# The last tile's chain in two column halves on VectorE, and the unpacking of a 4-bit matrix in another place

## What is computed

```python
c = attention(x, Wq, Wk, Wv, Wo, ...)              # 8 x 128 x 512
s = silu(c @ w_gate.T)                             # 1376 columns
s[the 688 columns of each row with the smallest |s|] = 0
x = x + (s * (c @ w_up.T)) @ w_down.T              # "x1" below
y = x @ weight[adapter_id].T                       # adapter, one of 16 matrices per batch
x = x + y @ W.T + b                                # W, b unpacked: (packed >> 4 & 15, packed & 15) - 8, times a scale
```

## Time and profile before

| | us |
|---|---|
| median of 3 runs (range) | 1464.77 (1464.52 to 1466.59) |
| the profiled execution | 1462.63 |
| its span, first to last instruction | 1460.8 |
| TensorE busy | 1405.2 (96%) |
| VectorE busy | 1184.6 (81%) |
| ScalarE busy | 873.3 (60%) |
| GpSimd busy | 820.0 (56%) |
| mean granted TensorE clock, share of full | 0.989 |

### The profile page before, as it was taken

One profiled execution on the slowest core, in us unless ns is written; L12 is line 12 of the kernel. 1 busy time (PEld: TensorE's weight loads), 2 busy tenths in 40 slices (PEclk: granted clock), 3 DMA queues, 4 the chain that ended last, 5 costly groups with the idle time before them and its releaser, 6 DMA issues.

```text
span 1460.8 us, 22910 instructions
## 1 busy us (share of the span) xinstructions
PE 1405.2 (96%) x7720; PEld 1168.0 (80%) x7720; DVE 1184.6 (81%) x2568; ACT 873.3 (60%) x2218; POOL 820.0 (56%) x829
## 2 busy tenths in 40 slices
PE   4899999999999999999999999999999989999997
PEld 3788888888888888888888888888888776676663
DVE  9888888888898889888988898889899877666550
ACT  4667666767676767676766677667767732222221
POOL 7766666666666666666666666666666611221112
PEclk8999999999999999999999999999999999999998
DMA  5111211121112111111211121112021303111120
GB/s 201 55 40 30 73 59 30 31 75 59 33 31 73 58 30 59 46 58 33 72 33 58 30 73 29 59 32 69 30 70 31 112 1 131 56 44 59 44 80 14
DMA packets 26624, 80.41 MB, mean 55 GB/s; under 512 B 9506, under 2 KB 10530, under 8 KB 23042
## 3 DMA queue, kind: packets, MB, share of 16 engines
q1 hardware_dynamic: 10114, 45.29, 8.9%
q0 software_dynamic: 16384, 33.59, 8.0%
HBM read 76.74 MB, written 2.10 MB: 54 GB/s over the span
## 4 chain that ended last, share of the span: by engine, by line
PE 87%; DVE 9%; issue 2%; ACT 1%; POOL 0%; POOLq 0%; DVEq 0%; ACTq 0%
PE proj_ps L107 11%; PE proj_ps L109 9%; PE proj_ps L108 9%; PE turn_ps L694 8%; PE value_ps L107 5%; PE score_ps L107 5%; PE score_ps L109 5%; PE score_ps L108 5%; PE out_ps L858 5%; PE value_ps L109 5%; PE value_ps L108 4%; PE gu_ps L109 3%; PE gu_ps L107 3%; PE gu_ps L108 3%; PE turn_ps L663 2%; DVE probs L1338 2%
## 5 line engine op out<-in xcount | busy, mean ns | idle before, releaser
L507 POOL DMA_INDIRECT kg<-kc,idx x256 | 289.2, 1130 | 256.3 <-issue 248.9
L516 POOL DMA_INDIRECT vg<-vc,idx x256 | 252.9, 988 | 110.3 <-issue 62.1
L1047 ACT ACTIVATE pt_hi<-turn_ps 128x512 fp32r<-128x512 f32 x320 | 189.7, 593 | 205.3 <-PE turn_ps L694 199.9
L1363 DVE TENSOR_TENSOR pt_lo<-turn_ps,pt_hi 128x512 fp32r<-128x512 f32 x320 | 218.9, 686 | 65.6 <-ACT pt_hi L1047 65.4
L1041 ACT ACTIVATE probs<-probs,shift,rstd 128x640 f32<-128x640 f32 x256 | 233.9, 915 | 37.4 <-DVE shift L1329 36.9
L1338 DVE CUSTOM_DVE_ANT_0 probs<-score_ps,mask 128x640 f32<-128x640 f32 x256 | 209.3, 817 | 23.9 <-PE score_ps L109 22.7
L107 PE MATMUL proj_ps<-w_hi,xt_hi 128*128 128x512 f32 (+1 forms) x512 | 185.9, 363 | 19.8 <-POOL w_lo L483 11.0
L694 PE MATMUL turn_ps<-cst,probs 128*128 128x128 f32 x1280 | 191.8, 272 | 0.0
L694 PEld LDWEIGHTS turn_ps<-cst,probs 128*128 128x128 f32 x1280 | 159.5, 141 | 26.6
L109 PE MATMUL proj_ps<-w_hi,xt_lo 128*128 128x512 f32 (+1 forms) x512 | 175.0, 342 | 0.0
L108 PE MATMUL proj_ps<-w_lo,xt_hi 128*128 128x512 f32 (+1 forms) x512 | 174.4, 341 | 0.0
(11 more groups left out here) (202 smaller groups left out, 3211.2 us busy)
## 6 DMA issues: line engine op xcount, KB each, us to landing
w_raw<-wqkv SPq DMA_DIRECT2D x7, 1536.0 KB, 6.4
wo_raw<-wo SPq DMA_DIRECT2D x8, 1024.0 KB, 4.9
wa_sb<-wa SPq DMA_DIRECT2D x7, 1024.0 KB, 4.8
kg<-kc,idx POOLq DMA_INDIRECT x256, 2.7
vg<-vc,idx POOLq DMA_INDIRECT x256
wg_raw<-wg SPq DMA_DIRECT2D x2, 1376.0 KB, 5.9
wu_raw<-wu SPq DMA_DIRECT2D x1, 2752.0 KB
wd_sb<-wd SPq DMA_DIRECT2D x1, 2560.0 KB, 10.0
```

The lines of the kernel that those rows point to most:

```text
L507: pool.indirect_dma_start(kg[:, b % 2, c, :], None, kc, bass.IndirectOffsetOnAxis(ap=idx[:, b * NC + c:b * NC + c + 1], axis=0))\
L516: pool.indirect_dma_start(vg[:, b % 2, c, :], None, vc, bass.IndirectOffsetOnAxis(ap=idx[:, b * NC + c:b * NC + c + 1], axis=0))\
L1047: act.activation(pt_hi[:, (b + j) % 2, :], turn_ps[1 - j % 2][:, :], ACT.Copy)\
L1363: dve.tensor_tensor(pt_lo[:, at, :], turn_ps[1 - j % 2][:, :], pt_hi[:, at, :].bitcast(F32), ALU.subtract).then_inc(p_lo_done[j], 1)
```

## The change

Seven things are edited. Line numbers are those of the kernel before.

1. **The last tile from the down product on** runs in two halves of 256 of the 512 columns (`HALVES`), each in PSUM space of its own. `down_last(half)` does all 11 chunks on 256 columns. VectorE adds x straight out of PSUM (`add_x_last`, in place of ScalarE's copy and GpSimd's addition), and copies the turned x1 to a tensor of its own (`copy_x1_last` into `x1t_last`, so it waits for no bias). `adapter_last(half, from_half)` multiplies two of the four chunks for 256 columns. ScalarE copies y and rounds it straight out of PSUM (`copy_y_last`, `round_y_last`), VectorE subtracts (`split_y_last`). One VectorE operation, `finish_last`, does the scaling and the last addition.
2. **TensorE's order** in `last_tile` is rewritten around these halves.
3. **GpSimd** keeps for tile 7 only `add_bias_last`; its list is y_lo(6), add_bias_last, add_int4(6).
4. **`down(i)`** waits for jobs 0 and 1 of `copy_h` at chunk 0, and for job 2 only at chunk 8.
5. **`unpack(0)`** moves from step TAIL + 1 to step TAIL + 2, behind piece 4 and ahead of `split_o`.
6. **`unpack(1)` and `unpack_bias`** move out of phase 1, to the place between `drop_lower_half(0)` and `pick(1)` in phase 2. The small memset and its wait that ended `unpack_bias` stay in step TAIL + 1.
7. **The packed data** go to space that later holds `y`, `x1` and the first part of `ht`; their transfers wait for the turn of piece 4 in the step before the last.

```diff
-            pw_sb = h_sb0[:, 0:2 * DM].rearrange("p (a n) -> p a n", a=2).bitcast(I32)
-            pb_sb = h_sb0[:, 2 * DM:2 * DM + DM // 2].bitcast(I32)
+            packed_at = ht_at + NF * S * 4
+            pw_sb = nc.alloc_sbuf_tensor_at("pw_sb", [P, 2, DM], I32, offset=packed_at)[:, :, :]
+            pb_sb = ht[:, 0:2, :].rearrange("p c t -> p (c t)").bitcast(I32)
...
-                    sp.wait_ge(scored[REP - 1], STEPS)
+                    sp.wait_ge(p_turned[NJ - 1], STEPS - 1)
...
-                    sp.wait_ge(res_done, B)
+                    sp.wait_ge(res_last_done, 1)
...
                     def last_tile(i):
                         y_lo(i - 2)
                         add_int4(i - 2)
                         add_x(i - 1)
                         add_bias(i - 1)
-                        add_x(i)
-                        add_bias(i)
                         y_lo(i - 1)
+                        add_bias_last()
                         add_int4(i - 1)
-                        y_lo(i)
-                        add_int4(i)
...
+                    def down(i):
+                        for c in range(NF):
+                            width = FCH[c][1]
+                            if c == 0:
+                                wait(pe, h_copied[0], i + 1)
+                                wait(pe, h_copied[1], i + 1)
+                            elif c == 8:
+                                wait(pe, h_copied[2], i + 1)
...
+                    def down_last(half):
...
+                            last = pe.matmul(down_last_ps[half], hts[1][0:width, c, :],
+                                             wd_sb[0:width, c, HALVES[half]], start=(c == 0), stop=(c == NF - 1))
+                        last.then_inc(downed, 1)
+                    def turn_x1_last(half):
+                        wait(pe, x1_last_done, half + 1)
...
+                    def adapter_last(half, from_half):
+                        wait(pe, x1_last_copied, from_half + 1)
+                        pe.wait_ge(wa_last_in, 16)
+                        for k in (2 * from_half, 2 * from_half + 1):
+                            last = pe.matmul(adapted_last_ps[half], x1t_last[:, k * P:(k + 1) * P],
+                                             was[1][:, k, HALVES[half]], start=(k == 0), stop=(k == NK - 1))
...
+                    def turn_y_last(half):
+                        wait(pe, y_copied, B + half)
...
+                    def int4_last(half):
+                        wait(pe, yt_lo_last_done, half + 1)
+                        for c in (2 * half, 2 * half + 1):
+                            w, turn = wf[:, c // 2, c % 2, :], slice(c * P, (c + 1) * P)
+                            pe.matmul(out_pss[1], yt_his[1][:, turn], w, start=(c == 0), stop=False)
+                            last = pe.matmul(out_pss[1], yt_los[1][:, turn], w, start=False, stop=(c == NK - 1))
...
                         turn_x1(i - 1)
-                        down(i, range(NF // 2))
+                        down_last(0)
                         adapter(i - 1)
-                        down(i, range(NF // 2, NF))
+                        turn_x1_last(0)
+                        down_last(1)
                         turn_y(i - 1)
-                        turn_x1(i)
-                        adapter(i)
+                        adapter_last(0, 0)
+                        turn_x1_last(1)
+                        adapter_last(1, 0)
+                        adapter_last(0, 1)
+                        adapter_last(1, 1)
+                        turn_y_last(0)
                         int4(i - 1)
-                        turn_y(i)
-                        int4(i)
+                        turn_y_last(1)
+                        int4_last(0)
+                        int4_last(1)
...
                         copy_y(i - 1)
-                        copy_down(i)
                         split_y(i - 1)
-                        copy_x1(i)
-                        copy_y(i)
+                        for half in range(2):
+                            copy_y_last(half)
+                        round_y_last(0)
                         scale_int4(i - 1)
-                        split_y(i)
-                        scale_int4(i)
+                        round_y_last(1)
...
-                        if s == TAIL + 1:
-                            unpack(0)
...
-                        if s == TAIL + 1:
-                            unpack(1)
...
+                        if s == TAIL + 2:
+                            unpack(0)
                         if live(s):
                             split_o(s)
                         if s == TAIL + 1:
                             for k in WU_ON_DVE:
                                 split_up(dve, k)
-                            unpack_bias()
+                            dve.memset(many[:, :], 0.0).then_inc(cleared, 1)
+                            dve.wait_ge(cleared, 1)
...
+                    def finish_last():
+                        wait(dve, int4_done, B)
+                        wait(dve, x1b_done, B)
+                        dve.scalar_tensor_tensor(acc[:, B - 1, :], out_pss[1], scl[:, 0:1], xns[1][:, :],
+                                                 ALU.mult, ALU.add).then_inc(res_last_done, 1)
...
                     pick_edge(0)
                     drop_lower_half(0)
+                    unpack(1)
+                    unpack_bias()
                     for i in range(1, B):
                         pick(i)
                         times_up(i)
                         drop_lower_half(i)
+                    for half in range(2):
+                        add_x_last(half)
+                        copy_x1_last(half)
+                    for half in range(2):
+                        split_y_last(half)
+                    finish_last()
```

More of the change, by code:

```diff
@@ L347, in adaln_attn_ffn @@
             bias = place("bias", [DM])
+            ht_at = rest[0]
             ht = place("ht", [NF, S])
@@ L590, in tile, with add_bias_last @@
                             front(i + 2)
+                    def add_bias_last():
+                        wait(pool, x1_last_done, len(HALVES))
+                        pool.tensor_tensor(xns[1][:, :], x1s[1][:, :], bias[:, :], ALU.add).then_inc(x1b_done, 1)
                     def last_tile(i):
@@ L849, in turn_h @@
                         last.then_inc(h_turned[n], 1)
[L851 to L856, removed]
[L857 to L861 removed]
+                    def down(i):
+                        for c in range(NF):
+                            width = FCH[c][1]
+                            if c == 0:
[3 more added lines that the diff above has]
+                                wait(pe, h_copied[2], i + 1)
+                            last = pe.matmul(out_ps[:, :], ht[0:width, c, :], wd_sb[0:width, c, :],
+                                             start=(c == 0), stop=(c == NF - 1))
+                        last.then_inc(downed, 1)
@@ new lines, in down_last @@
+                    def down_last(half):
+                        for c in range(NF):
+                            width = FCH[c][1]
+                            if c == 0:
+                                wait(pe, h_copied[0], B)
+                                wait(pe, h_copied[1], B)
+                            elif c == 8:
+                                wait(pe, h_copied[2], B)
+                            last = pe.matmul(down_last_ps[half], hts[1][0:width, c, :],
+                                             wd_sb[0:width, c, HALVES[half]], start=(c == 0), stop=(c == NF - 1))
+                        last.then_inc(downed, 1)
@@ new lines, in turn_x1_last @@
+                    def turn_x1_last(half):
+                        wait(pe, x1_last_done, half + 1)
+                        for r in range(2):
+                            k = 2 * half + r
+                            last = pe.transpose(turn_last_ps[half][:, r * P:(r + 1) * P], x1s[1][:, k * P:(k + 1) * P],
+                                                ident)
+                        last.then_inc(x1_turned, 1)
+                    def adapter_last(half, from_half):
[4 more added lines that the diff above has]
+                                             was[1][:, k, HALVES[half]], start=(k == 0), stop=(k == NK - 1))
+                        if from_half:
+                            last.then_inc(adapted, 1)
@@ new lines, in turn_y_last @@
+                    def turn_y_last(half):
+                        wait(pe, y_copied, B + half)
+                        split = ys[1][:, :].rearrange("p (a q r) -> p a r q", a=2, r=2)
+                        for r in range(2):
+                            last = pe.transpose(turn_last_ps[half][:, r * P:(r + 1) * P], split[:, half, r, :], ident)
+                        last.then_inc(y_turned, 1)
+                    def int4_last(half):
[4 more added lines that the diff above has]
```

(11 more changed lines are left out.)

25 lines of the change are left out of this document (23 added, 2 removed).

## The result

| | before | after |
|---|---|---|
| median (range), us | 1465.68 (1464.52 to 1467.4), 4 runs | 1454.26 (1453.67 to 1457.5), 4 runs |
| profiled execution, us | 1462.63 | 1454.36 |
| its span, us | 1460.8 | 1452.6 |
| VectorE busy, us | 1184.6 | 1185.2 |
| GpSimd busy, us | 820.0 | 816.1 |

The ratio after / before is 0.9926 [0.9907, 0.9944]: the changed kernel is 11.4 us faster by the medians. The forecast was 1449.0 with a range of 1446.0 to 1454.0; the median lies 5.3 us above the forecast and 0.3 us above the range.

The account below looks back on a forecast made before the run. TensorE was taken to bound the kernel, busy at full clock except for a wait in step TAIL + 1 and the chain at the end. Gains 5.7 - 0.3 + 0.4 + 10.0 = 15.8 us gave a median of 1449.0, range 1446.0 to 1454.0.

Parts of the forecast that it names:

- A: Step TAIL + 1: with unpacking gone, TensorE's last values and project_o start earlier; 5.7 us gained.
- its two ends: Step TAIL + 1: 5.7 us if VectorE's second half of normalise goes first, 2.4 us if GpSimd does.
- the engine which is late by its recorded start has to wait: Step TAIL + 1: read from GpSimd's row stretched to 1.40 us; GpSimd is late here, so 5.7 us was taken.
- GpSimd gets in: Rival, step TAIL + 1: GpSimd runs between normalise's two halves, gain only 2.4 us, median 1452.3; chance 0.28.
- B: Tile 0: unpack(1) and bias start where pick(1) did and delay ScalarE's copies and `down`; cost 0.3 us.
- the gap's shrinking: Tile 0: unpacking might start earlier in VectorE's gap of 1.52 us, and then cost nothing.
- unpack(0): Step TAIL + 2, ahead of split_o: takes 1.8 us, fits in VectorE's 3.21 us wait for ScalarE; costs nothing.
- C: Split wait in `down`: gains 0.4 us at tile 6, nothing in tiles 1 to 5.
- D: The end: last tile in halves and new engine orders, at full clock; 10.0 us gained.
- the rival of rows that do not halve: The end: 256-column fp32 rows cost up to 0.44 us, giving 1461.6; chance 0.10, shared with some low clock.
- the clock rival: The end: TensorE's clock stays low, some 22 us of work doubles, 1471 us, slower than before; chance 0.03.
- the last wait: The end, ahead of the last half of int4: TensorE waits some 0.6 us for VectorE's second subtraction.

Follow-up runs that it names:

- e2: Kernel before with only the unpacking moved as in the change, old end and undivided wait in down; 1466.56 us, ratio 1.0011 to before.
- e4: Changed kernel with unpack(1) and the bias ahead of drop_lower_half(0) instead of behind it; 1451.18 us, ratio 0.9919 to before.
- e7: Changed kernel with the last tile's chain in one piece of 512 columns, TensorE's order adapted; 1456.8 us, ratio 0.9923 to before.
- e8: Changed kernel unaltered, run again for a second profile; 1455.59 us, ratio 0.9927 to before.
- e5: Changed kernel with ScalarE's high part of piece 4 ahead of split_up(2) in step TAIL + 1; 1451.89 us, ratio 0.9906 to before.
- e3: Changed kernel with GpSimd's last low part of wu (chunk 2) given to VectorE, behind split_o; 1448.92 us, ratio 0.9899 to before.
- e1: Changed kernel with unpacking and its transfers back in step TAIL + 1, new last tile and split wait kept; 1456.34 us, ratio 0.9943 to before.

## Why the prediction was wrong

**A failed, at the choice between its two ends.** The working had the pair start at 1169.27, its second half at 1169.74 and GpSimd at 1169.76, and decided for VectorE by 0.02 us. All three came within 0.02 us of that, shifted by the 1.1 us of phase 1: 1170.39, 1170.86 (the recorded start of the second half) and 1170.86. What failed is the sentence that the engine which is late by its recorded start has to wait. In the five profiles with this code (after, e2, e4, e7, e8) GpSimd's row begins 0.47 to 0.48 us behind the pair's, which is where the second half begins in the record, and each time GpSimd had its 3.11 to 3.12 us and the second half, recorded with 3.46 to 3.47 us, ended behind it. The row that was read as evidence, GpSimd's 1.40 us at 1150.33, says the same on a second look: it began inside the first half (1150.04 to some 1150.5), waited for the end of that half, ran to 1151.73, and the second half came after it. The two halves of that pair of 2.04 us, by themselves in the kernel before:

```profile
L1356 DVE TENSOR_SCALAR probs<-probs,recips x2: 545/1060/1575, 1150.0 to 1150.5; 128x640 f32<-128x640 f32 x2
```

The prediction had named this pair as what speaks for the rival, and had given the 0.02 us more weight. VectorE did not keep its place for its next instruction. So this was no tie to be decided by hundredths: it is enough for GpSimd to be there when the first half ends. e5 shows the other order, with 5.23 us. The Trainium skill (SBUF — State Buffer, Who interferes with whom) has the shared port pair go to whoever issues first for the whole instruction, and says that issue order decides. The trace agrees as far as each holder keeps it for a whole instruction (3.11 to 3.12 us unstretched, in all five); who had issued first is what the recorded starts do not tell when they lie 0.01 us apart.

The recorded rival **GpSimd gets in** had 2.4 us for this case. By the segments it is 2.44, 2.67 and 2.49 us in e8, e4 and e2, but 1.27 and 1.33 in the changed kernel's first profile and in e7, because there the low clock lasted longer behind the same wait. With the rival alone the median would have been 1452.3, inside the range.

**B was mis-sized:** 2.64 us for 0.3. Two terms were wrong. First, the start: the unpacking did not begin where pick(1) had started. VectorE's gap, "issue" in the rows, grew from 1.52 to 2.07 us, so that the unpacking began with TensorE's first turn of h and not 0.6 us ahead of it; `down` began 3.59 us behind that turn where it had begun 2.64 behind it (0.95 us, 0.3 expected). The prediction had held only the gap's shrinking for possible. In the six kernels with the unpacking in this place the gap is 2.00 to 2.46 us; what makes it is not shown. Second, the clock: the sum followed VectorE and ScalarE to `down`'s start and had no term for what idle time on TensorE does to the work behind it. `down` took 1.70 us more. Together 2.65. Without that fall B costs 0.9 us (e3) to 1.35 (e5); the 0.46 us between the two is the gap, 2.00 us in one and 2.46 in the other.

**What is open:** when idle time of about 2 us is followed by the low clock. It was in after, e7 and e8 (1.97 to 2.02 us idle) and in e2 (2.35), and it was not in e3 (1.92) and e5 (2.38), so it is not the length alone. In the four with the fall, step TAIL + 1 had a low stretch 40 us earlier, and in the two without it that stretch was absent; whether that, or the place of the wait in time, decides was not tried.

**unpack(0) was right:** it ran in 1.74 us from 1194.33 and left 1.64 us of VectorE's wait for ScalarE ahead of split_o, of the 3.21 in the earlier trace rows.

**C was right:** 0.44 us less wait in front of `down(6)`, 0.35 us in the segment, for 0.4.

**D was right:** 10.3 us for 10.0. Row by row: 0.22 us for 256 columns of fp32 (44 rows in 9.5 us, 16 adapter rows in 0.87 + 2.59 = 3.5 us), so the rival of rows that do not halve is out; clock 1.00, so the clock rival is out at this place; the last wait 0.36 us for 0.6; `finish_last` 0.75 for 0.69; 25.5 us from the first half's start to the end for 25.7. The last transfer was issued 1.4 us after that of tile 6, and from the end of VectorE's last operation (1449.35 + 0.75) to the end of the span it took 2.5 us; from GpSimd's last in before (1457.09 + 1.30) it was 2.4 us, so the two did not get in each other's way.

**The sum.** By the segments 1.27 - 2.64 + 0.35 + 10.32 = 9.3 us, and the profiled execution's 8.3 us is that less the 1.1 us by which `wu_lo` came later. The medians have 11.4 us. The difference of 2 us is within what the executions of one kernel differ by (1453.67 to 1457.5 here), and the profiled execution of before was 3.0 us below its median; which of its stages were quicker than usual no second profile of it shows.

## What to carry to other kernels

When VectorE and GpSimd can hold each other, don't decide an order by hundredths of the recorded starts: a row that is stretched includes its own wait, and a GpSimd instruction that is ready can get in between two VectorE instructions that stand back to back, so count the whole of its length in front of VectorE's next instruction where that is of a kind that was held here (normalise, the shift-and-mask; the subtractions out of PSUM were not). When a move leaves TensorE idle at a new place, carry the low clock behind it as a term of its own beside the idle time (here nothing to 2.5 us behind some 2 us). At the end of a kernel look first at which engines hand over to which and in what order (8.8 us here), and only then at cutting the work into halves (1.5 us).

## What was not expected of the hardware

- GpSimd's `wu_lo`, with a recorded start equal to that of VectorE's next instruction, ran unstretched in 3.11 to 3.12 us in five of five profiles, and VectorE's pair grew from 1.02 to 3.93 or 3.94 us. In e5 it began 0.22 us ahead of the second pair, while VectorE was at a subtraction out of PSUM (0.68 us, not stretched), and held that pair in the same way (3.75 us).
- Behind the same wait of 3.15 to 3.16 us the low clock reached from the last values to the first rows of project_o in one profile (to 1181) and over the gate product alone in another (some 1177 to 1180.3); the segment differed by 1.2 us.
- About 2 us of idle time on TensorE was followed by the low clock in four profiles and by none in two.
- A gap that the profile calls "issue" grew from 1.52 us to between 2.00 us (e3) and 2.46 us (e5) when another instruction of VectorE came to stand behind it; with the first instruction of `pick` left in its place it is 1.54 us (e1).
